# Streamed attention and feed-forward stage: layer norm's root moved from VectorE to GpSimd, and two projections moved behind scores and turn in odd steps

## What is computed

```python
def attn_layer(x, Wqkv, qs, ksc, Wo):
    q, k, v = split(x @ Wqkv)                 # 128 -> 3 x 1024
    q = l2norm(q) * qs
    k = l2norm(k) * ksc
    q = q * cos * scale + rotate_half(q) * sin * scale
    k = k * cos / scale + rotate_half(k) * sin / scale
    return local_attention(q, k, v) @ Wo      # softmax over 64 keys: own and previous window

def ffn_layer(x, g, bln, W1, b1, W2, b2):
    xn = (x - mean(x)) / sqrt(var(x) + 1e-05) * g + bln
    a, gate = split(xn @ W1 + b1)             # 128 -> 2 x 341
    return a * gelu(gate) @ W2 + b2

for i in range(6):
    x = attn_layer(shift_tokens(x), ...) + x
    x = ffn_layer(shift_tokens(x), ...) + x
```

## Time and profile before

| | us |
|---|---|
| median of 3 runs | 2929.43 (2925.14 to 2930.21) |
| the profiled execution | 2919.78 |
| its span | 2918.0 |

### The profile page before, as it was taken

How to read it: one execution, slowest core, us unless ns; L and a number is a source line. 1 busy time by engine, 2 the same in 40 slices (tenths; PEclk the granted TensorE clock), 3 DMA queues, 4 the chain that set the end, 5 groups by cost and what they waited for, 6 DMA issues and landing times. The chain is left out here.

```text
span 2918.0 us, 59125 instructions
## 1 busy us (share of the span) xinstructions
PE 2569.8 (88%) x20009; PEld 1646.7 (56%) x20009; DVE 1798.8 (62%) x4075; ACT 1551.6 (53%) x5035; POOL 1363.3 (47%) x1980
## 2 busy tenths in 40 slices
PE   5999978898989979867489997899999999999997
PEld 3455545465645646545345554566666666666665
DVE  3566656546657645555645555777777777777774
ACT  1455536525747636522145553566666666666654
POOL 0344434203536613300024443877777777777772
PEclk8799998999989989988679998999999999999998
DMA  2000000010000000000000001010100101011000
GB/s 69 1 0 0 0 8 2 12 33 5 2 4 2 2 32 0 1 5 8 2 26 0 0 0 50 19 34 20 32 25 27 38 20 31 23 31 34 19 24 8
DMA packets 45658, 47.14 MB, mean 16 GB/s; under 512 B 11947, under 2 KB 31413, under 8 KB 45430
## 3 DMA queue, kind: packets, MB, share of 16 engines
q1 hardware_dynamic: 45430, 44.18, 5.4%
HBM read 31.05 MB, written 0.52 MB: 11 GB/s over the span
## 5 line engine op out<-in xcount | busy, mean ns | idle before, releaser
L1025 POOL TENSOR_TENSOR l_probs<-l_probs,rowinv 128x512 f32<-128x512 f32 (+2 forms) x256 | 192.4, 772 | 570.9 <-DVE rowinv L1037 570.1
L2256 ACT ACTIVATE net_probs<-bank,net_negmax 128x96 f32<-128x96 f32 x768 | 250.9, 338 | 188.9 <-DVE net_negmax L2389 188.7
L1045 DVE TENSOR_REDUCE negmax<-scores 128x1 f32<-128x508 f32 (+4 forms) x512 | 212.8, 467 | 223.5 <-PE scores L922 179.6
L2318 POOL TENSOR_TENSOR net_probs<-net_probs,net_inverse 128x384 f32<-128x384 f32 x192 | 158.7, 827 | 233.3 <-DVE net_inverse L2385 233.3
L1025 POOL TENSOR_TENSOR lora_probs<-lora_probs,rowinv 128x508 f32<-128x508 f32 (+1 forms) x256 | 149.5, 617 | 251.4 <-DVE rowinv L1037 251.4
L2389 DVE TENSOR_REDUCE net_negmax<-bank 128x4 f32<-128x384 f32 x192 | 106.3, 554 | 238.8 <-PE bank L2091 238.1
L2310 POOL TENSOR_TENSOR net_rope<-net_rope,net_sin_parts 128x512 f32<-128x512 f32 x192 | 244.0, 1271 | 9.8 <-DVE net_sin_parts L2359 9.8
L990 ACT ACTIVATE l_probs<-scores,negmax 128x512 f32<-128x512 f32 (+2 forms) x256 | 139.5, 550 | 168.1 <-DVE negmax L1045 167.3
L124 DVE COPY turned<-flip 128x512 f32<-128x512 f32 (+3 forms) x280 | 163.0, 582 | 74.1 <-PE flip L949 64.7
L2328 POOL TENSOR_TENSOR net_rope<-net_rope,net_head_inv 128x512 f32<-128x512 f32 x192 | 201.2, 1048 | 0.0
L737 DVE TENSOR_REDUCE negmax<-scores 128x2 f32<-128x256 f32 (+2 forms) x192 | 157.7, 822 | 61.2 <-PE scores L645 33.4
(11 more groups left out here) (424 smaller groups left out, 6452.5 us busy)
## 6 DMA issues: line engine op xcount, KB each, us to landing
net_w_qkv<-in_L_ffn_Wqkv SPq DMA_DIRECT2D x12, 768.0 KB, 5.3
net_vals_between<-net_vals SPq DMA_DIRECT2D x48, 192.0 KB, 2.5
net_w_out<-in_L_ffn_Wo SPq DMA_DIRECT2D x6, 512.0 KB, 4.2
net_vals_between<-net_vals SPq DMA_DIRECT2D x48, 64.0 KB, 1.9
moe_w<-in_L_ffn_w13T SPq DMA_DIRECT2D x8, 256.0 KB, 2.7
net_w<-in_L_ffn_W SPq DMA_DIRECT2D x6, 341.0 KB
moe_w<-in_L_ffn_w2T SPq DMA_DIRECT2D x8, 128.0 KB, 2.3
ctx_tok<-in_ctx SPq DMA_DIRECT2D x1, 768.0 KB, 6.5
```

The lines of the kernel that those rows point to most:

```text
L1025: last = nc.gpsimd.tensor_tensor(own, own, rowinv[:, u * tail + w:u * tail + w + 1].to_broadcast([P, k1 - k0]), ALU.mult)
L1045: last = nc.vector.tensor_reduce(negmax[:, u * tail + w:u * tail + w + 1], scores[:, 2 * qt + h, k0:k1], AX.X, ALU.max, negate=True)
L2256: last = nc.scalar.activation(prob_blocks(g)[:, w, :], score_blocks(g)[:, w, :], ACT.Exp, bias=maxima[:, g % 4, w:w + 1], accum_out=sums[: ...
L2318: nc.gpsimd.tensor_tensor(prob_blocks(g), prob_blocks(g), part, ALU.mult).then_inc(shared.sem, 1)
```

## The change

Four edits:
1. On DVE `root_of_variance` is gone. DVE now makes two small results from the statistic: `ln_sum`, the variance with the epsilon added, and `ln_shift`, the mean times -1. Both raise `spread_in`.
2. On POOL, in the step after (`LATE + 1`, step 6), behind share and scaling and ahead of the addition, `inverse_root` runs on `ln_sum`, 14 operations on [128, 2], and a 15th multiplies `ln_shift` by `ln_inv`. ACT's norm of z in step 7 waits for that one, as before for DVE's.
3. On PE, in odd steps, the projections of k and of values come behind scores and turn. Even steps keep q in front. Their waits are the same.
4. A tile `ln_sum` of [128, 2] is added.

ACT's and SP's lists are the same.

The diff:

```diff
--- before.py
+++ after.py
@@ -1809,7 +1809,7 @@
                 HB = BANK // DH
                 head_sums, head_inv = sbl("head_sums", [P, 2, QT * 2 * HB]), sbl("head_inv", [P, 2, QT * 2 * HB])
                 head_temp = sbl("head_temp", [P, 3, QT * 2 * HB])
-                ln_inv, ln_shift, ln_temp = sbl("ln_inv", [P, QT]), sbl("ln_shift", [P, QT]), sbl("ln_temp", [P, 3, QT])
+                ln_sum, ln_inv, ln_shift, ln_temp = sbl("ln_sum", [P, QT]), sbl("ln_inv", [P, QT]), sbl("ln_shift", [P, QT]), sbl("ln_temp", [P, 3, QT])
                 qk_T = sbl("qk_T", [P, 2, 2, N])
                 probs = sbl("probs", [P, 3, 4 * (KEYS + DH)])
                 flat_p = sbl("probs_turned", [P, 3, BANK])
@@ -1838,7 +1838,7 @@
                         nc.gpsimd.memset(acts[D // 2:P, 2, :], 1.0).then_inc(made.sem, 1)
 
                 stream(p, GT, (rope, sin_parts, squares, vals, mid), (w_qkv, w_out, w1, w2, vec), (qk_rows, sines, cosines, sin_table, cos_table),
-                       (head_sums, head_inv, head_temp), (ln_inv, ln_shift, ln_temp), (qk_T, probs, flat_p, maxima, sums, inverse, window16),
+                       (head_sums, head_inv, head_temp), (ln_sum, ln_inv, ln_shift, ln_temp), (qk_T, probs, flat_p, maxima, sums, inverse, window16),
                        (late, znT, gelu, acts))
 
         by_batch = lambda v: v.rearrange("p (b n) -> p b n", b=B)
@@ -1889,7 +1889,7 @@
             w_qkv, w_out, w1, w2, vec = weights
             qk_rows, sines, cosines, sin_table, cos_table = tables
             head_sums, head_inv, head_temp = heads_norm
-            ln_inv, ln_shift, ln_temp = ln
+            ln_sum, ln_inv, ln_shift, ln_temp = ln
             qk_T, probs, flat_p, maxima, sums, inverse, window16 = softmax
             late, znT, gelu, acts = ffn
             INNER, HB, BLOCKS, QB = H * DH, BANK // DH, 4, N // 4
@@ -1916,8 +1916,8 @@
             out_made, out_added = signal("net_out_made", JOBS), signal("net_out_added", JOBS)
             low_moved, late_made, late_moved = signal("net_low_moved", JOBS), signal("net_late_made", JOBS), signal("net_late_moved", JOBS)
             measured, gathered = signal("net_measured", 2 * JOBS), signal("net_gathered", 2 * JOBS)
-            LN_OPS = 11
-            ln_rooted, normed = signal("net_ln_rooted", LN_OPS * JOBS), signal("net_normed", 2 * JOBS)
+            spread_in = signal("net_spread", 2 * JOBS)
+            ln_rooted, normed = signal("net_ln_rooted", ROOT_OPS * JOBS), signal("net_normed", 2 * JOBS)
             ln_shifted = signal("net_ln_shifted", JOBS)
             z_turned, z_moved = signal("net_z_turned", JOBS), signal("net_z_moved", JOBS)
             gates_made, gates_moved = signal("net_gates_made", JOBS), signal("net_gates_moved", 3 * JOBS)
@@ -2063,21 +2063,6 @@
                             until(pe, parted, 2 * u - 1)
                             nc.tensor.matmul(qk_bank[0], xnT[:, (QT * b + t) * P:(QT * b + t + 1) * P], w_qkv[:, half_cols(c)],
                                              start=True, stop=True).then_inc(q_filled.sem, 1)
-                        u = at_tick(s, PROJ + 1, 2, S)
-                        if u is not None:
-                            m, c, t = step_of(u)
-                            l, b = job(m)
-                            own = xnT[:, (QT * b + t) * P:(QT * b + t + 1) * P]
-
-                            until(pe, parted, 2 * u)
-                            nc.tensor.matmul(qk_bank[1], own, w_qkv[:, INNER + c * BANK:INNER + (c + 1) * BANK],
-                                             start=True, stop=True).then_inc(k_filled.sem, 1)
-
-                            until(pe, stored, min(G, s - VALUES))
-                            until(pe, v_copied, u)
-                            nc.tensor.matmul(v_bank, own, w_qkv[:, 2 * INNER + c * BANK:2 * INNER + (c + 1) * BANK],
-                                             start=True, stop=True).then_inc(v_filled.sem, 1)
-                            values_in = u + 1
                         g = s
                         if 0 <= g < G:
                             until_copied(pe, g)
@@ -2103,6 +2088,21 @@
                                     last = nc.tensor.transpose(turn_bank[:, (k * QT + q) * P:(k * QT + q + 1) * P],
                                                                rope[:, m % 3, q, k, cols_of(c)], ident[:, :])
                             last.then_inc(turned.sem, 1)
+                        u = at_tick(s, PROJ + 1, 2, S)
+                        if u is not None:
+                            m, c, t = step_of(u)
+                            l, b = job(m)
+                            own = xnT[:, (QT * b + t) * P:(QT * b + t + 1) * P]
+
+                            until(pe, parted, 2 * u)
+                            nc.tensor.matmul(qk_bank[1], own, w_qkv[:, INNER + c * BANK:INNER + (c + 1) * BANK],
+                                             start=True, stop=True).then_inc(k_filled.sem, 1)
+
+                            until(pe, stored, min(G, s - VALUES))
+                            until(pe, v_copied, u)
+                            nc.tensor.matmul(v_bank, own, w_qkv[:, 2 * INNER + c * BANK:2 * INNER + (c + 1) * BANK],
+                                             start=True, stop=True).then_inc(v_filled.sem, 1)
+                            values_in = u + 1
                         g = s - FLIP
                         if 0 <= g < G:
                             pe.wait_ge(shared.sem, shared.at(0, g + 1))
@@ -2330,6 +2330,12 @@
                         if j is not None:
                             pool.wait_ge(reduced.sem, reduced.at(0, 2 * j + 2))
                             inverse_root(pool, head_sums[:, j % 2, :], 1e-24, head_inv[:, j % 2, :], head_temp, rooted, ROOT_OPS * j)
+                        n = at_tick(s, LATE + 1, PER, JOBS)
+                        if n is not None:
+                            pool.wait_ge(spread_in.sem, spread_in.at(0, 2 * n + 2))
+                            inverse_root(pool, ln_sum[:, :], LN_EPS, ln_inv[:, :], ln_temp, ln_rooted, ROOT_OPS * n)
+                            pool.wait_ge(ln_rooted.sem, ln_rooted.at(0, ROOT_OPS * (n + 1)))
+                            nc.gpsimd.tensor_tensor(ln_shift[:, :], ln_shift[:, :], ln_inv[:, :], ALU.mult).then_inc(ln_shifted.sem, 1)
                         u = at_tick(s, PROJ + 1, 2, S)
                         if u is not None:
                             add_parts(u, 0)
@@ -2358,25 +2364,6 @@
                         table = sin_table[:, l % 2, t, s:s + 1, :].rearrange("p o (f d) -> p o f d", f=2).to_broadcast([P, HB, 2, DH // 2])
                         nc.vector.tensor_tensor(sin_parts[:, (2 * u + s) % 4, :].rearrange("p (h f d) -> p h f d", f=2, d=DH // 2), swapped, table,
                                                 ALU.mult).then_inc(parted.sem, 1)
-
-                    def root_of_variance(dve, n):
-
-                        lower, y, t = ln_temp[:, 0, :], ln_temp[:, 1, :], ln_temp[:, 2, :]
-                        done = [LN_OPS * n]
-
-                        def then(ins):
-                            done[0] += 1
-                            ins.then_inc(ln_rooted.sem, 1)
-                            dve.wait_ge(ln_rooted.sem, ln_rooted.at(0, done[0]))
-                        then(nc.vector.tensor_scalar(lower, meanvar[:, 0:QT, 1], LN_EPS, -0.5, ALU.add, ALU.mult))
-                        then(nc.vector.tensor_scalar(y.bitcast(I32), lower.bitcast(I32), -0.5, ROOT_MAGIC, ALU.mult, ALU.add))
-                        for r in range(3):
-                            then(nc.vector.tensor_tensor(t, y, y, ALU.mult))
-                            then(nc.vector.tensor_tensor(t, t, lower, ALU.mult))
-                            then(nc.vector.scalar_tensor_tensor(y if r < 2 else ln_inv[:, :], t, 1.5, y, ALU.add, ALU.mult))
-                        assert done[0] == LN_OPS * (n + 1)
-
-                        nc.vector.scalar_tensor_tensor(ln_shift[:, :], meanvar[:, 0:QT, 0], -1.0, ln_inv[:, :], ALU.mult, ALU.mult).then_inc(ln_shifted.sem, 1)
 
                     for s in TICKS:
                         g = s - 1
@@ -2443,7 +2430,9 @@
                                 dve.wait_ge(measured.sem, measured.at(0, 2 * n + q + 1))
                                 nc.vector.bn_aggr(meanvar[:, q, :], stats[:, q, :]).then_inc(gathered.sem, 1)
                             dve.wait_ge(gathered.sem, gathered.at(0, 2 * n + 2))
-                            root_of_variance(dve, n)
+
+                            nc.vector.tensor_scalar(ln_sum[:, :], meanvar[:, 0:QT, 1], LN_EPS, None, ALU.add).then_inc(spread_in.sem, 1)
+                            nc.vector.tensor_scalar(ln_shift[:, :], meanvar[:, 0:QT, 0], -1.0, None, ALU.mult).then_inc(spread_in.sem, 1)
                         m = at_tick(s, SHIFT, PER, JOBS)
                         if m is not None:
                             l, b = job(m)
```

## The result

The changed kernel takes 2969.53 us (median of 4 runs, 2963.33 to 2974.9), against 2927.45 for the kernel before on the same chip. The ratio is 1.0137, interval 1.0111 to 1.0162: 42 us slower. The forecast was slower by 50 us, 2979, and the range 2952 to 3004 holds the result.

What follows compares the result with a forecast made beforehand. The last stage was taken as close to bound by PE, with PE's idle waits to win. +41 in the jobs, +7 ahead and +2 at the end took 2919.8 to 2970, plus 9.6 to 2979 us; range 2952 to 3004.

Steps and rivals of the forecast that it cites:

- the root's end moved it to the transpose of z: Step 7 on PE: the 2.24 us wait at values goes, but POOL's root ending at 2310.4 delays z; no gain.
- 15 operations on POOL at 0.28, 4.2 us: Norm's root on POOL in step 6: 15 two-element operations at 0.28 each including waits, 4.2 us, between 3.0 and 5.0.
- A bare pair of steps is a loop of 10.2 us: Even plus odd step: chain through DVE's copy, PE's turn and k, and ACT takes 10.2 us; no pair can be shorter.
- The waits of one job: PE's walk through eight steps: 2.8 us of waits go, 4.7 come, so a job gets 1.9 us longer.
- k at 0.97 in its new place: PE's projection of k, odd steps: length 0.97 us, read from step 5 before the change and used behind the turn.
- the 41 us: Steps with both the second half's work and projections: 1.9 us more per job over 21.4 jobs, +41 us.
- Ahead of the first output projection +7: The 11 steps ahead, with bare pairs: +1.3 us a pair over 5 pairs, +7 us.
- The end +2: Last job: root on the path with nothing beside it, 4.2 + 0.4 us instead of at most 3.2; +2 us.
- PE-bound: Copies of the turned reach PE in time, all 2.8 us of waits per job go: 2870 us; chance 0.07.
- The root as the long pole (3007): POOL's root takes 5 us or more, norming z late; at 5.9 it is +28, 3007 us; chance 0.12.
- The forecast added 9.6: Step from the profiled execution to the median of the runs: 9.6 us, taking 2970 to 2979.

Runs made afterwards that it cites:

- version 1: Kernel before with only norm's root moved to POOL, PE's order as before: 2938.81 us, ratio 1.0042.
- version 6: Kernel before with norm's root on POOL in two Newton rounds instead of three, and heads' root of step 5 moved to end of step 4: 2887.74 us, ratio 0.9869.
- version 2: Kernel before with only PE's new order, k and values behind scores and turn in odd steps, root left on DVE: 3023.42 us, ratio 1.0322.
- Version 3: Changed kernel with DVE's copy of the turned q and k directly behind the row maximum: 2950.07 us, ratio 1.0071.
- versions 5: Kernel before with norm's root on POOL, and heads' root of step 5 moved to end of step 4 on POOL: 2918.51 us, ratio 0.9955.
- version 4: Changed kernel with ACT's exp and copy of the turned ahead of k's square, copy of values and norm of z, odd steps: 3017.99 us, ratio 1.0302.
- copy first, early: Changed kernel with DVE's copy of the turned behind the maximum and heads' root of step 5 at end of step 4: 2925.47 us, ratio 0.9995.

## Why the prediction held, point by point

- **Values' wait gone, and the root's end moved it to the transpose of z.** Right, and shown by version 1: 2.08 at values became 2.14 at the transpose, period 44.25 against 44.2 to 44.4.
- **15 operations on POOL at 0.28, 4.2 us.** Measured 0.276 each, 4.14. The operations by themselves, from the list of tile `net_ln_temp` (count, ns min/median/max), leave some 0.08 for each wait between them:

```profile
L1867 POOL TENSOR_TENSOR net_ln_temp<-net_ln_temp x72: 193/193/194, 1924.1 to 2946.5; 128x2 f32<-128x2 f32 x72
```

  The Trainium skill's ratio ("GPSIMD Engine Reference", Performance versus the Vector engine), which it gives for 2048 elements, didn't carry over to two: 193 ns here stand against 161 for DVE's same product before the change, 1.2 times and not 1.96. The measurement decides.
- **A bare pair of steps is a loop of 10.2 us.** Measured 10.02 (scores at 1881.57, 1891.58 and 1901.59), against 8.83 before: 1.19 more, forecast 1.3.
- **The waits of one job.** From the rows above, each counted by the delay of PE's start, which is 0.06 or more above the idle time in brackets (scores (7): the last sum starts at 2333.32, scores without a wait follow 0.22 later, so 2333.54 to 2334.81):

| | forecast | measured |
|---|---|---|
| scores (6) | 0.2 | 0.1 |
| scores (7) | 1.3 | 1.27 |
| transpose of z | 1.2 | 1.18 |
| scores (9) | 0.65 | 0.63 |
| ups, step 2 | some tenths | 0.46 |
| scores (11) | 1.05 | 1.03 |
| gone | 2.74 | 2.74 |
| a plain job longer by | 1.9 | 1.4 |

- **The term that was mis-sized in the jobs: k at 0.97 in its new place.** Every wait has its forecast size and the sum, 4.67 less 2.74, is 1.93. Yet a plain job is only 1.4 longer. The term I had taken over without a look is k's own length, 0.97 from its start to that of values. This is the length behind the weighted sums. Behind the turn it takes 0.86 (2336.33 to 2337.19; the same in steps 1, 3 and 5). Four a job make 0.44, and 1.93 less 0.44 is 1.49, so the 41 us should have been some 31. Of these, 25.8 show in the 21 jobs; the kernel before had two longer jobs (45.99 and 45.71, at a granted clock of 0.96) that account for 3 of the difference, and six of 44.4.
- **Ahead of the first output projection +7, measured 12.7.** From the first scores to those of step 4, six pairs of steps, PE took 61.2 instead of 53.4, which is 7.8 more and close to the forecast 7, though 3.4 us at a lower clock in the first pair (1851.0 to 1854.4) are in it. A bare pair alone is 1.19 longer, as above. The other 4.9 come before the first scores, a term that the sum put at nothing. There PE's first turn waits for POOL's scaling, and until now k and values stood in front of it and filled that time. Now they stand behind it: the wait shown is 6.31 instead of 3.85, but the turn came only 1.4 later, counted from the first projection; the scores came 3.6 later still, of which k and values make 1.7. Much of the rest is clock, since the turn and k ran at 1.2 GHz:

```profile
1841.39 1.11 PE L2088 MATMUL bank<-ident,net_rope 128*128 128x128 f32 x4 [6.31 <-POOL net_rope L2328]
1842.30 1.91 PE L2098 MATMUL bank<-net_w_qkv,xnT 128*128 128x512 f32 x2
```

  The clock fell at 1837.3, while PE waited for POOL. In version 1, with the old list on PE, the first scores came 2.4 later than before at a lower clock alone. So the order makes most of the 12.7 (after less root only 10.5, order only less before 10.6), and some 2 differ between executions.
- **The end +2, measured 5.2.** The transpose of z in the last job waited 6.56 instead of 4.39: the root with nothing beside it is 2.2 longer, which is the forecast +2. The rest is in the job ahead, which took 29.5 instead of 26.8 from its output projection to the last one, and there it is nearly all clock. PE waits 2.7 for the activations in both kernels, but in the changed one the granted clock falls to 1.2 GHz in that wait, at 2929.6, and the ups and the down projection run at it. Before, then after:

```profile
2886.30 1.13 PE L2179 MATMUL bank<-net_znT,net_w 128*128 128x256 f32 x4 [2.71 <-DVE net_acts L2398]
2888.49 1.58 PE L2190 MATMUL bank<-net_w,net_acts 128*128 128x128 f32 x12 [0.46 <-DVE net_acts L2456]
...
2930.32 2.08 PE L2179 MATMUL bank<-net_znT,net_w 128*128 128x256 f32 x4 [2.70 <-DVE net_acts L2385]
2933.45 2.90 PE L2190 MATMUL bank<-net_w,net_acts 128*128 128x128 f32 x12
```

  From the start of the ups to the last output projection it is 6.64 instead of 4.37, so 2.3 of the 2.7. It differs between executions: that job took 26.1 in version 6 and 27.9 in version 2, and 28.3 to 30.3 in the others. Why the clock fell there in one execution and not in another isn't shown. Version 1, in the old order, has 3.9 of the 5.2.
- **The rivals.** PE-bound needed the copy within 2.9 to 3.5 us of scores; it was there at 4.1 (2330.66 to about 2334.75). Version 3, in which it is there in time, shows what that was worth: 1.66 us a job. The root as the long pole (3007) is excluded by 4.14.
- **From the profiled execution to the median.** The forecast added 9.6, the distance that the kernel before had. The changed kernel's median (2969.5) is only 1.3 above its profiled execution (2968.2), so no run bears that term out.

By terms, then: +26 in the jobs against 41, +13 against 7, +5 against 2, and +5 ahead of the stage, which no edit made. The mechanism held, wait by wait. That the sum came within 8 us is partly luck: the jobs were put too high by 15, and in the profiled execution the start, the end and the part ahead of the stage, with more time at a lower clock among them, made up for nearly 14 of that.

## What to carry to other kernels

When work is moved on the busiest engine's queue, look at what it had been covering: here two projections, 1.8 us together, hid a copy on another engine, and moved behind their neighbour they hid nothing. Price two edits together if the one changes what the other has to be in time for; the root's move cost 9 us in one order and gave 54 in the other. The chain of tiny dependent operations cost its count times the step from one to the next on either engine, 0.28 us on POOL and some 0.20 on DVE, so fewer steps and an earlier start (versions 5 and 6) won what moving it could not.

## What the runs showed of the hardware

A tiny operation of DVE can be held until a POOL operation ends. In version 4 `net_ln_sum`, one input in SBUF, took 0.98 in the median of 24 (here 2314.87 to 2315.85) and ended with POOL's addition; in the changed kernel it never took more than 0.17:

```profile
2314.55 1.27 POOL L2310 TENSOR_TENSOR net_rope<-net_rope,net_sin_parts 128x512 f32<-128x512 f32 x1
```

In the kernel before the same happened to a product of the root, which has two inputs in SBUF: 161 ns in the median, but 1133 and 1187 at most, and in the job of the earlier trace rows it ended with POOL's addition (2303.29 to 2304.42, the addition 2303.13 to 2304.40). The Trainium skill ("SBUF — State Buffer", Who interferes with whom) says that DVE and GpSimd share a pair of ports, that a DVE instruction with two inputs in SBUF contends with a GpSimd one that reads SBUF, and that for a DVE instruction in a mode that uses both ports whoever issues first gets the pair for the whole instruction, the other being fully blocked. Both rows look like that; in which mode the one with a single input ran, no run shows. So part of what DVE's root cost was POOL's addition, about 1 us of its 3.2.

PE's granted clock fell in single jobs of version 1, which waits over 2 us at once at the transpose of z. Two pairs of jobs took 47.21 and 45.83 in place of 44.25, and the stretches (us, then busy time of PE, PEld, DVE, ACT, POOL, then the granted clock) show 0.92 and 0.96 where full is 2.4 GHz, so part of these stretches ran at 1.2:

```profile
2480.00:2525.00 45.00, 42.31 (x395) 29.52 (x395) 31.07 (x64) 28.84 (x102) 34.64 (x67) 1.00 0.11 31
2525.00:2570.00 45.00, 42.30 (x369) 28.36 (x368) 28.11 (x58) 27.33 (x91) 35.28 (x70) 0.92 0.05 13
2570.00:2615.00 45.00, 42.30 (x376) 28.72 (x375) 30.11 (x61) 28.33 (x99) 33.82 (x67) 0.96 0.07 19
```

The profiled executions of all versions can be put side by side: the longest wait of PE in each of the 21 jobs, and how many of these jobs had a granted clock below full.

| | longest wait of PE in a job | jobs below full clock |
|---|---|---|
| before | 2.1 to 2.2 | 2 |
| after | 1.2 | 0 |
| root only | 2.1 | 5 |
| order only | 3.3 to 3.5 | 3 |
| DVE copy first | 2.2 | 4 |
| ACT exp first | 1.8 to 2.2 | 13 |
| heads' root early | 1.4 | 0 |
| early, two rounds | 0.4 | 0 |
| copy first, early | 1.5 | 0 |

In these jobs every fall of the clock lies in such a wait or within 1.7 us behind its end, and the jobs with one were 0.4 to 3 us longer. But most waits of 2 us and more were followed by no fall, the longest waits don't have the most, and in the last jobs the clock also fell at waits of 1.5. So versions with shorter waits also lost less to the clock in these executions; that the length of a wait alone decides isn't shown.
